# A PE loop with one signal a tile and a register of its own, stores cut and spread in another way, and a fifth tile loaded ahead, in a kernel for packed lower triangles of Gram matrices

## What is computed

```python
def _L0_rec_ref(inputs):
    Z = jnp.einsum('bnd,bmd->bnm', inputs, inputs)
    n = inputs.shape[1]
    li, lj = jnp.tril_indices(n, k=-1)
    return Z[:, li, lj]
```

## Time and profile before

| | |
|---|---|
| median of 3 runs | 411.94 us (411.42 to 413.04) |
| the profiled execution | 411.66 us, of which the span of the program is 409.9 us |
| PE (matmuls) busy | 378.6 us, 92% of the span |
| PE weight loads busy | 371.8 us, 91% |
| DVE busy | 367.1 us, 90% |
| POOL busy | 197.7 us, 48% |
| ACT busy | 177.5 us, 43% |
| moved by DMA | 151 MB, 368 GB/s over the span |
| the chain that ended last | PE 88%, issue 4%, DVE 3%, ACTq 2%, ACT 1%, DMA 1% |

### The profile page before, as it was taken

One profiled execution on the slowest core, in us unless ns is written; L12 is line 12 of the kernel. 1 busy time (PEld: TensorE's weight loads), 2 busy tenths in 40 slices (PEclk: granted clock), 3 DMA queues, 4 the chain that ended last, 5 costly groups with the idle time before them and its releaser, 6 DMA issues.

```text
span 409.9 us, 68720 instructions
## 1 busy us (share of the span) xinstructions
PE 378.6 (92%) x33024; PEld 371.8 (91%) x33024; DVE 367.1 (90%) x240; ACT 177.5 (43%) x821; POOL 197.7 (48%) x974
## 2 busy tenths in 40 slices
PE   4589999999999999999999999999999999999950
PEld 4588999999999999999999999999999999999950
DVE  3328999999999999999999999999999999999965
ACT  0101245444455444555444546434555443555184
POOL 1000074663818274472818366381827457281845
PEclk9999999999999999999999999999999999999995
DMA  7259999999999999999999999999999999995407
GB/s 307 66 211 426 423 421 421 421 422 421 418 425 422 423 421 422 421 422 422 420 414 367 423 383 399 406 395 423 383 422 365 421 398 423 404 374 238 119 20 202
DMA packets 21291, 151.01 MB, mean 368 GB/s; under 512 B 2705, under 2 KB 2833, under 8 KB 4881
## 3 DMA queue, kind: packets, MB, share of 16 engines
q1 hardware_dynamic: 18752, 135.77, 82.1%
q10 hardware_dynamic: 2512, 14.97, 9.5%
HBM read 134.22 MB, written 16.52 MB: 368 GB/s over the span
## 4 chain that ended last, share of the span: by engine, by line
PE 88%; issue 4%; DVE 3%; ACTq 2%; ACT 1%; DMA 1%; DVEq 0%
PE bank_set L297 88%; ACTq L154 2%; DMA x_in<-x_dram 1%; DVE packed_rows L147 1%; DVE x_in L248 1%; DVE x_turned L224 1%; ACT products L324 1%; ACT packed_rows L142 1%; ACT packed_rows L136 0%; DVE packed_rows L136 0%; DVE x_turned L253 0%; DVEq L76 0%; DVEq L223 0%; ACTq L315 0%; DVEq L273 0%
## 5 line engine op out<-in xcount | busy, mean ns | idle before, releaser
L297 PE MATMUL bank_set<-x_turned 32*64 32x64 f32 x33024 | 378.6, 236 | 18.0 <-issue 9.1
L297 PEld LDWEIGHTS bank_set<-x_turned 32*64 32x64 f32 x33024 | 371.8, 132 | 24.7 <-issue 20.4
L224 DVE STREAM_TRANSPOSE x_turned<-x_in 128x2048 f32<-128x2048 f32 x128 | 293.1, 2293 | 33.2 <-DMA x_in<-x_dram 21.1
L147 POOL COPY packed_rows<-row_halves 32x32 f32<-32x32 f32 (+30 forms) x930 | 190.1, 204 | 202.1 <-DVE row_halves L241 164.5
L324 ACT COPY products<-bank_set 128x512 f32<-128x512 f32 (+1 forms) x91 | 68.5, 759 | 189.0 <-PE bank_set L297 170.9
L241 DVE STREAM_TRANSPOSE row_halves<-products 128x1024 f32<-128x1024 f32 x60 | 72.2, 1204 | 0.0
L142 ACT COPY packed_rows<-row_halves 128x128 f32<-128x128 f32 x240 | 53.5, 299 | 19.7 <-issue 19.0
L136 ACT COPY packed_rows<-row_halves 128x32 f32<-128x32 f32 (+30 forms) x465 | 60.8, 219 | 0.2 <-DVE row_halves L241 0.2
L324 ACT ACT_TABLE_LOAD x1 | 1.3, 1283 | 17.4 <-PE bank_set L297 17.4
L248 DVE STREAM_TRANSPOSE x_in<-products 128x512 f32<-128x512 f32 (+1 forms) x5 | 4.8, 999 | 4.0 <-ACT products L324 4.0
L147 POOL COPY packed_rows<-x_in 32x32 f32<-32x32 f32 (+30 forms) x31 | 4.9, 209 | 4.4 <-DVE x_in L248 4.4
## 6 DMA issues: line engine op xcount, KB each, us to landing
x_in<-x_dram SPq DMA_DIRECT2D x128, 1024.0 KB, 17.1
y_dram<-packed_rows ACTq DMA_DIRECT2D x21, 504.0 KB, 8.9
y_dram<-packed_rows ACTq DMA_DIRECT2D x7, 252.0 KB
y_dram<-packed_rows ACTq DMA_DIRECT2D x28, 63.0 KB
y_dram<-packed_rows SPq DMA_DIRECT2D x2, 504.0 KB, 4.8
y_dram<-packed_rows SPq DMA_DIRECT2D x1, 380.0 KB
y_dram<-packed_rows ACTq DMA_DIRECT2D x1, 380.0 KB
y_dram<-packed_rows SPq DMA_DIRECT2D x1, 124.0 KB
```

Source lines behind the costliest of these rows:

```text
L147: return copy(packed_rows[first:first + BLOCK, group % 2, :, at + BLOCK:at + i], halves(group)[first + BLOCK:first + HALF, i, :, 0:i - BLOCK])
L224: nc.vector.transpose(x_turned[:, j].rearrange("p c b s (h u n v) -> p u v (c b s h) n", h=ROWS // BLOCK, u=PAIRS, v=PAIR), x_in[:, k]).th ...
L297: done = nc.tensor.matmul(bank_sets[s][side * HALF:(side + 1) * HALF, g, at, :].rearrange("r (n u v) -> r u n v", u=PAIRS, v=PAIR), rows, ...
```

## The change

**PE.** Only the last matmul of a tile signals, once, so all waits on `tile_multiplied` count tiles. The loop is written with labels and a register `count`, which the waits read directly; it is raised by 3 (one lap) ahead of the last 64 matmuls of the lap, not at the loop's end. Because the later of the two waits on `kept` now meets the raised value, both `kept` semaphores start at 3 (`LAP`), where before only `kept[1]` did.

**Stores.** The odd groups 1 to 11 are still cut into 32, 16 and four times 4 lanes, but the four 4-lane DMAs no longer follow at once: one is issued behind each of the next four copies out of PSUM that has no whole store behind it. Group 13 goes as two DMAs of 32 lanes.

**Loads.** Tiles 0 to 3 load at once; tile 4 waits until tile 0 has been multiplied and tile 5 until tile 1 has.

```diff
--- before.py
+++ after.py
@@ -33,8 +33,7 @@
     IN_RING = 8
-    LATE = {3: 0, 4: 1}
-    ARRAY_TILES = QUADRANTS * SIDES
+    LATE = {4: 0, 5: 1}
     LAP = 3
@@ -64,11 +63,10 @@
     LAST_HOME = (GROUPS * PIECES - 2) * 4 + 2
-    FEW = 4
+    FEW, FEW_UNTIL = 4, GROUPS - 4
     WHOLE_SIDES = [(side, 0, BLOCK) for side in range(SIDES)]
-    BY_FEW = [(0, 0, BLOCK), (1, 0, BLOCK // 2)] + [(1, q, q + FEW) for q in range(BLOCK // 2, BLOCK, FEW)]
-    LANES = [WHOLE_SIDES, BY_FEW]
-    STORES = [len(lanes) * 16 for lanes in LANES]
+    FIRST_LANES = [(0, 0, BLOCK), (1, 0, BLOCK // 2)]
+    FEW_LANES = [(1, q, q + FEW) for q in range(BLOCK // 2, BLOCK, FEW)]
     x_joined = x.rearrange("b (i r) d -> (b i) (r d)", r=JOINED)
@@ -123,10 +121,18 @@
         def piece_rows(piece):
             return slice(ROWS - (piece + 1) * PIECE, ROWS - piece * PIECE)
+        def by_few(group):
+            return group % 2 == 1 and group <= FEW_UNTIL
+        def stores_before(group):
+            return sum(16 * len(FIRST_LANES + FEW_LANES if by_few(g) else WHOLE_SIDES)
+                       for g in range(group % 2, min(group, GROUPS - 1), 2))
         def wait_packed_free(engine, group):
             if group >= 2:
-                engine.wait_ge(stored[group % 2], group // 2 * STORES[group % 2])
+                engine.wait_ge(stored[group % 2], stores_before(group))
         def halves(group):
             return last_halves if group == GROUPS - 1 else row_halves
@@ -175,24 +181,24 @@
                     sync.wait_ge(turned[j], (lap + 1) * LAP)
                 elif t in LATE:
                     lap, j = place(LATE[t])
-                    sync.wait_ge(tile_multiplied[j], (lap + 1) * ARRAY_TILES)
+                    sync.wait_ge(tile_multiplied[j], lap + 1)
                 sync.dma_start(x_in[:, k], x_joined[t * PARTS:(t + 1) * PARTS]).then_inc(loaded[k], 16)
             for t in range(TILES):
                 load(t)
             sync.wait_ge(packed_home, (GROUPS - 1) * PIECES)
             sync.wait_ge(packed_across, (GROUPS - 1) * LONG_PIECES)
-            store(sync, GROUPS - 2, slice(0, PACKED), LANES[(GROUPS - 2) % 2])
+            store(sync, GROUPS - 2, slice(0, PACKED), WHOLE_SIDES)
             store_last(sync, 0)
             for b in range(2):
-                groups = len(range(b, GROUPS - 1, 2))
                 last = 2 * len(WHOLE_SIDES) * 16 if (GROUPS - 1) % 2 == b else 0
-                sync.wait_ge(stored[b], groups * STORES[b] + last)
+                sync.wait_ge(stored[b], stores_before(GROUPS + b) + last)
         @block.gpsimd
         def _(pool):
-            pool.sem_inc(kept[1], LAP)
+            for s in range(SETS):
+                pool.sem_inc(kept[s], LAP)
             for j in range(BLANK):
                 nc.gpsimd.memset(x_turned[:, j, CHUNKS // 2:CHUNKS], 0.0).then_inc(turned[j], LAP - 1)
             for group in range(GROUPS):
@@ -220,7 +226,7 @@
                 k, (lap, j) = t % IN_RING, place(t)
                 dve.wait_ge(loaded[k], (t // IN_RING + 1) * 16)
                 if lap > 0:
-                    dve.wait_ge(tile_multiplied[j], lap * ARRAY_TILES)
+                    dve.wait_ge(tile_multiplied[j], lap)
                 nc.vector.transpose(
                     x_turned[:, j].rearrange("p c b s (h u n v) -> p u v (c b s h) n", h=ROWS // BLOCK, u=PAIRS, v=PAIR),
                     x_in[:, k]).then_inc(turned[j], LAP)
@@ -232,7 +238,7 @@
                     lap, j = place((group + 1) * GROUP_TILES - 1)
                     s = set_of(j)[0]
-                    dve.wait_ge(kept[s], (lap + 1 + s) * LAP)
+                    dve.wait_ge(kept[s], (lap + 2) * LAP)
                 if group > 0:
                     dve.wait_ge(packed_home, n - PIECES + 1)
@@ -280,16 +286,21 @@
         @block.tensor
         def _(pe):
-            def multiply(j, step):
-                pe.wait_ge(turned[j], step)
+            count = nc.alloc_register(pe.engine, "count")
+            def multiply(j):
+                pe.wait_ge(turned[j], count)
                 s, in_set = set_of(j)
                 for slot in range(SLOTS):
                     at = in_set * SLOTS + slot
+                    if j == LAP - 1 and slot == SLOTS - 1:
+                        pe.reg_add(count, count, LAP)
                     for c in range(CHUNKS):
                         if in_set == SET_TILES[s] - 1 and slot == SLOTS - 1 and c == CHUNKS - 2:
-                            pe.wait_ge(kept[1 - s], step)
+                            pe.wait_ge(kept[1 - s], count)
                         for g in range(QUADRANTS):
                             for side in range(SIDES):
                                 rows = x_turned[g * BLOCK:(g + 1) * BLOCK, j, c, slot, side]
@@ -300,19 +311,23 @@
                                     rows,
                                     rows.rearrange("d (h u e) -> d u h e", h=ROWS // BLOCK, u=PAIRS),
                                     start=c == 0, stop=c == CHUNKS - 1)
-                                if c == CHUNKS - 1 and slot == SLOTS - 1:
-                                    done.then_inc(tile_multiplied[j], 1)
-            with pe.Fori(LAP, (LAPS + 1) * LAP, LAP) as step:
+                done.then_inc(tile_multiplied[j], 1)
+            pe.reg_mov(count, LAP)
+            pe.br("lap")
+            with nc.body("lap", valid_engines=[pe.engine]):
                 for j in range(LAP):
-                    multiply(j, step)
+                    multiply(j)
+                pe.br_lt(count, (LAPS + 1) * LAP, on_true="lap", on_false="laps_done")
+            nc.switch_bb("laps_done")
         @block.scalar
         def _(act):
             def keep(lap, s):
                 j = SET_TILES[0] * s
-                act.wait_ge(tile_multiplied[j + SET_TILES[s] - 1], (lap + 1) * ARRAY_TILES)
+                act.wait_ge(tile_multiplied[j + SET_TILES[s] - 1], lap + 1)
                 begin = lap * LAP + j - BLANK
                 t, end = max(0, begin), begin + SET_TILES[s]
                 while t < end:
@@ -349,16 +364,22 @@
             def store_whole(group):
                 act.wait_ge(packed_home, (group + 1) * PIECES)
                 act.wait_ge(packed_across, (group + 1) * LONG_PIECES)
-                store(act, group, slice(0, PACKED), LANES[group % 2])
+                store(act, group, slice(0, PACKED), FIRST_LANES if by_few(group) else WHOLE_SIDES)
             n = 0
             stores = 0
+            few = 0
             for lap in range(LAPS):
                 for s in range(SETS):
                     keep(lap, s)
                     if n >= (stores + 1) * PIECES * 4:
                         store_whole(stores)
                         stores += 1
+                        few = len(FEW_LANES) if by_few(stores - 1) else 0
+                    elif few > 0:
+                        store(act, stores - 1, slice(0, PACKED), FEW_LANES[-few:][:1])
+                        few -= 1
                     while n + PACK_LAG < (lap * LAP + (SET_TILES[0] if s == 0 else LAP) - BLANK) * 2:
                         pack(n)
                         n += 1
```

## The result

The changed kernel takes 407.01 us (median of 6 runs, 406.59 to 408.54), where the kernel before took 412.42 us in the same session. The ratio is 0.9873, with a 95% interval of 0.9848 to 0.9898. By the ratio that is 5.2 us less, and the interval leaves 4.2 to 6.3. The forecast was 404.5 us (400 to 410).

The account below looks back on a forecast made before the run. PE was taken as the bound, with the loads next. Earlier landings and group 13's two issues start DVE's last four transposes at 390.3, not 397.5: 7.2 us less than the profiled 411.66, so 404.5 us (400 to 410).

Parts of the forecast that it names:

- What bounds the kernel: PE sets the pace at 2.93 us a tile; loads, at 3.03 us in the later half, are the next bound.
- the sum: PE's lap could fall to about 8.33 us; at the end, DVE's last four transposes start 7.2 us earlier, at 390.3.
- the signs to look for: DVE waits for DMA later; beat near 8.45 us in the first third, then 8.8 to 9.1; tile 127 near 382.
- Signals and loop: In PE's loop, fewer signals save 0.15 us at two borders a lap, and the loop's end saves 0.15 us.
- A fifth tile ahead: At the loads' start, tile 3 fills an idle stretch, so every later landing moves 2.5 us forward, tile 127 to 381.9.
- rival 3: At the start, tile 3's load delays PE's code, so the stream starts 4.1 us later: 408.6 us, chance 0.05.
- the loads' pace stays: For the stores: bytes and DMAs are the same but for group 13, so the loads run as fast as before.
- Group 13 and the end: Two issues take about 0.8 us where six held ACT for 6.96; DVE's last transposes no longer wait for ACT.
- rival 1: Faster turning lets loads go earlier, and DVE becomes the bound at 8.44 us a lap: 395 us, chance 0.12.
- rival 2: PE gains nothing in the loop and stays the bound; half of DVE's 3.98 us wait returns: 409.7 us, chance 0.05.
- rival 4: ACT waits for the small DMAs and PE for ACT: mild 406 to 410 us, slower 413 to 421, chance 0.04 each.
- DVE's floor: From its busy share of 96.15 of 100, DVE needs 8.44 us a lap, 2.81 us a tile.

Follow-up runs that it names:

- Experiments 1: The kernel before with only the PE part of the change (one signal a tile, register, addition ahead of the last 64 matmuls): 409.67 us, ratio 0.9933.
- experiment 7: The changed kernel without the stores of groups 0 to 13 (14.5 MB not written): 390.2 us, ratio 0.9491.
- experiments 11: The changed kernel with eight signals a tile as before, its own register kept: 406.89 us, ratio 0.9902.
- 12: The kernel before with one signal a tile, its own loop kept: 409.11 us, ratio 0.9955.
- experiments 3: The changed kernel with the loads' start as before (tile 3 waits for tile 0, tile 4 for tile 1): 407.62 us, ratio 0.988.
- 8 to 10: The changed kernel with tiles 0 to 4, tiles 0 to 5, or no load held back for a tile: 405.1, 403.78 and 407.42 us.
- experiment 4: The changed kernel with the four 4-lane DMAs of each odd group issued at once, as before: 407.4 us, ratio 0.9877.

## Why the prediction was right, and where it was off

**What bounds the kernel** was read rightly: the loads stood close behind PE, and took over. Waits of DVE for loads appeared, the chain became DMA and DVE, the beat fell to 8.29 us (the sum had 8.33, the signs to look for said 8.45) and was 8.95 on average between 200 and 350 us, from 12868 passes in 150 us (forecast 8.8 to 9.1). Experiments 1, 7 and 11 show it in three ways.

**Signals and loop**: 0.15 us for each border and 0.15 for the loop's end were taken; 0.15 to 0.17 and 0.15 to 0.19 were measured, and the prediction's open question, wait or signals, is answered: the signals. That this would hardly come back as time was right as well.

**A fifth tile ahead** is the term that was mis-sized. The step "every later landing moves 2.5 us forward, tile 127 to 381.9" failed; it landed at 384.5. Most of the loss was priced among the rivals (rival 3: tile 3's load delays PE's code, given 0.05) and set to nothing in the sum, because the code was fetched beside loads and without. The kernel before showed the price: its first stop, beside the loads of tiles 0 to 2, was 3.43 us, the next ones 1.2 to 1.7. It happened once, not twice: the second stop grew by 2.3 us. The step said that the stream starts at the same event; it does, but that event moved. Tile 5 landed 0.8 us earlier than before and not 2.5 (DVE starts on it at 31.69, before at 32.48). The other 0.9 us were lost on the way, by "the loads' pace stays": tile 64 landed 3 us later than before, tile 127 only 0.1 later. The parts of tile 64 show where: its first landed 0.6 us earlier than before, its last 3.0 later. With the GB/s equal, the engines that are ahead took more of the total for a while, and the late ones less. Why that is so, no run shows. The result of 407.0 lies between the forecast and rival 3's 408.6; the range held it because it was made wide enough for that rival.

**Group 13 and the end** were right: 0.80 us of issues, DVE without a gap, its last four transposes 8.6 us behind the last landing where 8.4 were forecast. The sum missed by the landing, 2.6 us, and by hardly anything else.

**The rivals.** The loads follow (rival 1): the beat did not hold in the second half. PE gains nothing (rival 2): the beat fell by 0.5 us. ACT waits for the small DMAs (rival 4): the wait came, four times and 15.5 us in all where six times some 4 us were expected, and between 60 and 370 us PE did not wait for ACT, as worked out.

**DVE's floor** was put at 8.44 us a lap from its busy share. Without stores the program kept 8.3 with DVE busy all the time (experiment 7), so the floor was put too high by about 2%. The forecast did not rest on it; rival 1's 395 did, and would have been lower.

## What to carry to other kernels

When three queues are busy for nine tenths, ask of each what it would do if the first became quicker. Here the bytes moved in equal stretches (413 and 412 GB/s) and the landing of the last load (384.4 and 384.5 us) show that DMA was at its limit before the change already, so that 0.5 us taken off each of 42 laps brought only 2.7 us. A gain on such a kernel is then found where the limiting queue stands idle, at the start and the end: two more tiles ahead, beside a stop that is paid for anyway, bring 1.9 us by the ratios, more than the spreading of stores and the fifth tile together. And work on shares (which lanes go by which DMA) can be worth more than any instruction saved: whole stores cost 10.4 us against the change, all groups cut 12.6. To see which way to go, look at how far apart the parts of one load land: a total in GB/s does not tell five late parts from one.

## What the runs showed of the hardware

- Eight semaphore signals on the last matmuls of a tile stop PE by 0.15 to 0.17 us more than one signal does (experiments 11 and 12). The Trainium skill ("TensorE: Matmul & The Clock Gate", The cost: per-tile semaphore tail) gives 26.3 ns a signal, by which seven would be, as an estimate, 0.18 us; the runs come a little lower.
- PE's waits for code in its first lap are 1.1 to 1.9 us long with at most one load of 1 MB on the DMA engines, and 3.1 to 4.6 us with several queued; one long stop covers up to three further loads (experiments 3 and 8 to 10).
- The 16 parts of a load don't land together here. With stores in equal shares one part was on average 12 us behind the fifteenth; with 20% of the 1024 stored lanes sent by 4-lane DMAs four parts were 12 to 17 us behind the first; with 9% (the changed kernel) five were late, by 8 to 14. Against these 9%, sending 0% so costs 10.4 us and 20% costs 12.6, by the ratios. Without the stores up to group 13 the parts landed within 2.2 us on average.
- Clock: from 8 to 29 us it was granted at half (1.2 GHz) in the changed kernel's profile and at full (2.4 GHz) in experiment 4's, after the same 223 passes and a stop from 5.6 us on in both. A piece of 128 passes took 2.25 us at either level, so no difference shows there.
